# A 32-tile attention loop in eights, written out to all 32 tiles

## The reference

```python
def attn_layer(x, Wqkv, qs, ksc, Wo):
    q, k, v = jnp.split(x @ Wqkv, 3, -1)          # 16 heads of 64
    q = l2norm(q) * qs
    k = l2norm(k) * ksc
    q = q * cos * scale + rotate_half(q) * sin * scale
    k = k * cos * inv + rotate_half(k) * sin * inv
    out = local_attention(q, k, v)                # windows of 32, one back
    return out @ Wo
```

## Time and profile before

| | |
|---|---|
| median of 3 runs | 3703.05 us (3699.27 to 3705.26) |
| the profiled execution's own time | 3708.02 us |
| its span, first to last instruction | 3706.2 us |
| mean granted TensorE clock | 0.947 of full |
| busy: PE, DVE, ACT, POOL | 90%, 72%, 72%, 65% |

### The profile page before, as it was taken

One profiled execution on the slowest core, in us unless ns is written; L12 is line 12 of the kernel. 1 busy time (PEld: TensorE's weight loads), 2 busy tenths in 40 slices (PEclk: granted clock), 3 DMA queues, 4 the chain that ended last, 5 costly groups with the idle time before them and its releaser, 6 DMA issues. The chain is left out here.

```text
span 3706.2 us, 118376 instructions
## 1 busy us (share of the span) xinstructions
PE 3346.1 (90%) x42076; PEld 2217.8 (60%) x42076; DVE 2650.5 (72%) x4986; ACT 2678.7 (72%) x9257; POOL 2404.5 (65%) x2342
## 2 busy tenths in 40 slices
PE   5699998889999789999789999978999977999987
PEld 4466665656666556566566666655666655666656
DVE  6677786577778567778558777756787756777865
ACT  3388887378888458888638888836888854888873
POOL 3577776467777357677547777746777745777764
PEclk8799999899999899999889999989999989999999
DMA  2000001100000100000110000010000010000011
GB/s 67 10 7 7 7 7 32 25 8 7 7 7 5 46 15 7 7 7 7 35 23 7 7 7 6 9 43 14 7 7 7 6 41 18 7 7 7 7 31 42
DMA packets 141063, 57.76 MB, mean 16 GB/s; under 512 B 118598, under 2 KB 137668, under 8 KB 139460
## 3 DMA queue, kind: packets, MB, share of 16 engines
q1 hardware_dynamic: 140484, 50.01, 5.7%
HBM read 22.57 MB, written 2.10 MB: 7 GB/s over the span
## 5 line engine op out<-in xcount | busy, mean ns | idle before, releaser
L1524 POOL TENSOR_TENSOR qk_rot<-by_cos,by_sin 128x1024 f32<-128x1024 f32 x384 | 904.2, 2376 | 234.2 <-PE ring L558 146.2
L1321 ACT ACTIVATE probs<-s_ps,nbias 128x64 f32<-128x64 f32 x3072 | 942.7, 340 | 2.4 <-DVE nbias L1043 2.2
L1001 DVE TENSOR_TENSOR by_cos<-qk_ps,rotary 128x1024 f32<-128x1024 f32 x378 | 463.2, 1225 | 491.6 <-ACT squares L1307 491.6
L612 PE MATMUL ring<-wvo,xsT 128*32 128x512 f32 x6144 | 788.2, 606 | 0.0
L1321 ACT ACTIVATION_READ_ACCUMULATOR probs<-s_ps,nbias 128x1 f32 x3072 | 719.8, 234 | 0.0
L1542 POOL TENSOR_TENSOR qk_rot<-qk_rot,rnorm 128x1024 f32<-128x1024 f32 x192 | 365.7, 1905 | 419.4 <-DVE rnorm L748 419.4
L1513 POOL TENSOR_TENSOR probs<-probs,rrow 128x256 f32<-128x256 f32 x768 | 455.1, 614 | 275.7 <-DVE rrow L988 275.7
L1307 ACT ACTIVATE squares<-qk_ps 128x1024 f32<-128x1024 f32 x378 | 387.3, 1025 | 280.3 <-PE qk_ps L546 280.3
L558 PEld LDWEIGHTS ring<-cst,qk_rot 128*128 128x128 f32 x3072 | 342.8, 140 | 197.0 <-ACT vo L1144 165.8
L1004 DVE TENSOR_TENSOR by_sin<-qk_ps,rotary 128x1024 f32<-128x1024 f32 x378 | 459.2, 1215 | 0.0
L1016 DVE TENSOR_REDUCE sumsq<-squares 128x16 f32<-128x1024 f32 x384 | 455.2, 1185 | 0.0
(11 more groups left out here) (166 smaller groups left out, 5636.7 us busy)
## 6 DMA issues: line engine op xcount, KB each, us to landing
qk_rot<-L_ffn_Wqkv SPq DMA_DIRECT2D x7, 1024.0 KB, 5.0
xs<-x_tok SPq DMA_DIRECT2D x194, 32.0 KB
xs<-x_tok SPq DMA_DIRECT2D x194, 31.8 KB
by_cos<-x_tok SPq DMA_DIRECT2D x48, 128.0 KB
by_cos<-x_tok SPq DMA_DIRECT2D x48, 127.0 KB
wv<-L_ffn_Wqkv SPq DMA_DIRECT2D x7, 512.0 KB, 6.4
wo_pad<-L_ffn_Wo SPq DMA_DIRECT2D x14, 256.0 KB, 7.4
xs<-x_tok SPq DMA_DIRECT2D x194, 0.2 KB
```

The costliest lines, as they stand in the source:

```text
L612: last = mm(r[WIN * mh:WIN * (mh + 1), :], xsT[:, a, WIN * w:WIN * (w + 1)], wvo[:, mh, :, :], start=True, stop=True)
L1001: v.tensor_tensor(heads(by_cos[:, n, :]), heads(projection_banks(qk, k, it, s)), table.unsqueeze(1).broadcast_to([P, H, D]), ALU.mult)
L1321: last = nc.scalar.activation(probs[:, a, h // 4, :, h % 4, :], s_ps[:, half, c:c + 2 * WIN].rearrange("p (s c) -> p s c", s=2), ACT.Exp, ...
L1524: g.tensor_tensor(qk_rot[:, n, :], by_cos[:, n, :], by_sin[:, n, :], ALU.add).then_inc(added[qk], 1)
```

## The change

`schedule` keeps its loop only for the opening block, with two steps a turn as before. The attention of a layer is laid out by a new function, `every_tile`, which has no loop: 35 steps on PE, DVE and ACT and 33 on POOL are written out one after another. Every `step` of the attention loses its `it` argument, tile numbers become `NT * l + k`, and the bank waits come from `last_use` throughout. The order of the operations, their tiles, engines and shapes stay as they were, and so do SP's program, the FFN, and the loop over the layers. The code of a layer's attention grows from 19 to 35 steps on PE, DVE and ACT, and from 17 to 33 on POOL.

```diff
-        def schedule(loop, step, depth, n=NT, after_loop=None, before_last=None, turn=TPB):
-            turns = (n - depth) // turn
+        def schedule(loop, step, depth, n, after_loop=None):
+            turns = (n - depth) // 2
             for k in range(depth):
                 step(k, k % 2, None)
             with loop(0, turns) as it:
-                for r in range(turn):
+                for r in range(2):
                     step(depth + r, (depth + r) % 2, it)
...
+        def every_tile(step, depth, before_last=None):
+            for k in range(NT + depth):
+                if before_last and k == NT + depth - 1:
                     before_last()
-                step(k, k % 2, None)
+                step(k)
+
+        def tile_numbers(l, k):
+            return k, NT * l + k
...
                     def bank(use, s):
-                        i = ring_names.index(use)
                         b = ring_bank((par - s) % 2, use)
-                        if it is not None:
-                            name, s2, ago = use_before(i)
-                            freed(name, T0 - s2 - ago)
-                            if ago and k == 3 and last_use[b][0] != name:
-                                freed(*last_use[b])
-                        else:
-                            if last_use[b]:
-                                freed(*last_use[b])
-                            last_use[b] = use, T0 - s
+                        if last_use[b]:
+                            freed(*last_use[b])
+                        last_use[b] = use, T0 - s
                         return ring[:, b, :]
...
-                schedule(pe.Fori, step, 3, after_loop=after_loop)
+                every_tile(step, 3)
...
-                schedule(dve.Fori, step, 3, before_last=lambda: normalised(0, 0))
+                every_tile(step, 3, before_last=lambda: normalised(0, 0))
...
-                schedule(act.Fori, step, 3, before_last=w1_upper)
+                every_tile(step, 3, before_last=w1_upper)
...
-                schedule(pool.Fori, step, 1)
+                every_tile(step, 1)
```

More of the change, by code:

```diff
@@ L315, in schedule @@
             with loop(0, turns) as it:
-                for r in range(turn):
+                for r in range(2):
                     step(depth + r, (depth + r) % 2, it)
-            k = depth + turn * turns
+            k = depth + 2 * turns
             if after_loop:
@@ L465, in step @@
                     wv_transposed(1, 0)
-            schedule(pe.Fori, step, 4, turn=2, n=NG)
+            schedule(pe.Fori, step, 4, n=NG)
             for r in range(2, WVO_ROUNDS):
@@ L529, in project @@
                     def project(qk, n, s):
-                        if not there(k, it, s):
+                        if not there(k, None, s):
                             return
@@ L575, in scores @@
                     def scores(half, s):
-                        if not there(k, it, s):
+                        if not there(k, None, s):
                             return
-                        t, T, a = t0 - s, T0 - s, (par - s) % 2
+                        T, a = T0 - s, (par - s) % 2
                         first = (k - s) % TPB == 0
@@ L912, in step @@
                 stack_input(5)
-            schedule(dve.Fori, step, 6, turn=2, n=NG)
+            schedule(dve.Fori, step, 6, n=NG)
             with dve.Fori(0, DEPTH) as l:
@@ L1232, in first_wqk_upper @@
                     wqk_upper(0, part)
-            schedule(act.Fori, step, 4, turn=2, n=NG, after_loop=first_wqk_upper)
+            schedule(act.Fori, step, 4, n=NG, after_loop=first_wqk_upper)
             for r in range(2, WVO_ROUNDS):
@@ L1239, in _, with step @@
             with act.Fori(0, DEPTH) as l:
-                def step(k, par, it):
-                    t0, T0 = tile_numbers(l, k, it)
+                def step(k):
+                    (t0, T0), par = tile_numbers(l, k), k % 2
                     def q_evacuated(half, s):
-                        if not there(k, it, s):
+                        if not there(k, None, s):
                             return
@@ L1496, in _, with step @@
             pool.wait_ge(w0_in, 128)
-            schedule(pool.Fori, step, 4, turn=2, n=NG, after_loop=first_weights)
+            schedule(pool.Fori, step, 4, n=NG, after_loop=first_weights)
             step(NG + 4, 0, None)
             with pool.Fori(0, DEPTH) as l:
-                def step(k, par, it):
-                    t0, T0 = tile_numbers(l, k, it)
+                def step(k):
+                    (t0, T0), par = tile_numbers(l, k), k % 2
                     def normalise(half, s):
-                        if not there(k, it, s):
+                        if not there(k, None, s):
                             return
```

43 lines of the change are left out of this document (16 added, 27 removed).

## The result

The changed kernel takes 3640.05 us, the median of 4 runs (3639.45 to 3640.58), where the kernel before, run beside it, took 3701.91 (3699.27 to 3705.26): a ratio of 0.9832, 95% interval 0.9815 to 0.9849. The forecast was 3639.6.

What follows compares the result with a forecast made beforehand. PE, full inside the attention, was taken as the bound. From the 3703.05 us median, 63.4 us for twelve taken PE branches came off, all other terms zero: 3639.6 us, range 3632 to 3646, chance 90%.

Steps and rivals of the forecast that it cites:

- The edges' price: PE's two taken attention-loop branches a layer, twelve in all, cost 63.4 us of stall and lower clock, 5.3 each.
- the lower sum: The twelve PE edges built from idle time plus the half-clock share: 61.7 us, the low end of the saving.
- the twelve edges are of fixed length: PE's attention-loop edges are events of fixed length, so the saving was taken unchanged off the 3703.05 us median.
- The upper sum: The twelve PE edges built from every branch in full plus the clock share: 70.3 us, the high end.
- The other engines' edges: Attention-loop branches on ACT, DVE and POOL: losses lie under PE's stall or within full PE time, so removal wins zero.
- Registers and the loop's set-up: Removing the attention loop's fall-through branch, moves, additions and DVE address registers wins zero, covered by a full PE.
- New fetching: Fetching 16 more steps of straight attention code per engine costs zero; DVE and POOL add some 45 packets in all.
- Rival A: DVE's and POOL's straight attention code is fetched too late, 164 us come back, 3804 us; chance 3%.
- Waits, DMAs: In the attention no wait is added and no DMA moved, so nothing queues behind anything new.
- The layer branch: The layer loop's branch, 4.43 us on PE and taken five times, stays, its target further away: zero change.
- B: The small FFN loops start to miss, giving back 61 us, 3701 us, no change; chance 3%.
- C: TensorE's clock does not stay up in the unbroken attention, losing 41 us, 3680 us, a smaller gain; chance 4%.

Runs made afterwards that it cites:

- Experiment 1: The kernel before, its attention loop entered for two turns of eight steps instead of three, the third turn's steps written out: 3672.76 us, ratio 0.9919.
- experiment 2: The kernel before with six, four or two steps a turn instead of eight: 3725.89, 3836.59 and 3641.55 us; two steps give 78 taken branches.
- experiment 4: The loop of eight kept on some engines, the others written out: PE alone 3700.67 us; DVE, ACT, POOL 3657.62; ACT alone 3655.33; DVE and POOL 3639.70.
- experiment 6: The changed kernel with the loop over the six layers written out too, on all five engines: 3619.42 us, ratio 0.9780.

## Why the prediction was right, point by point

1. *The edges' price, 63.4 us from the starts of line 527.* Right: 64.0 us went from just these intervals, and the medians fell by 61.9 (63.0 against the median shown with the prediction). Experiment 1 halves it with the number of edges. The parts are right too: in these intervals PE was idle for 38.7 us before and for none after, and busy for 25.4 us longer (2436.3 against 2410.9), where the lower sum had 37.9 and 23.8.

The premise that the twelve edges are of fixed length was wrong. The branches of the profiled execution lasted from 3.63 to 5.05 us, and the runs of the kernel before spread over 6.0 us where those of the changed one spread over 1.1. The median of the kernel before itself came out between 3699.36 and 3703.05 us beside the different experiments. That forecast and result lie 0.45 us apart is therefore partly luck; an agreement within 3 or 4 us was what the method could promise.

The upper sum, 70.3 us from whole branches and the clock share, was too high as the text said, and so would be a sum by the Trainium skill's rule for throttled time ("TensorE: Matmul & The Clock Gate", Terms) laid on top of the branches' full durations: what handed-over matmuls cover has to come off.

2. *The other engines' edges lie under PE's: zero.* Right, and the mirror run with PE alone looped shows it (1.0001). The reading behind it was weaker: the 45 ns of ACT's branch record do not say that ACT loses little. On ACT the stall stands behind that record, as its sequencer's two records at the first edge of the kernel before show, 2.5 us apart:

```profile
L315 ACTq COMPARE_BRANCH  x1: 45/45/45, 304.2 to 304.2; - x1
L315 ACTq FUSED_REGOPS  x1: 127/127/127, 306.7 to 306.7; - x1
```

What the text left out is the price of these edges without PE's cover: 15 to 17 us for ACT's, nothing for DVE's and POOL's. A change that wrote out only PE would have been predicted 17.6 us too low (3657.62 against 3640.05).

3. *Registers and the loop's set-up: zero.* Right: the 78 held edges of experiment 2 with all their register work leave PE full, and the 1.5 us that this kernel takes longer are its 288 matmuls more.

4. *New fetching: zero, with some 45 new packets.* The zero is right, the count was not: the second queue went from 211 to 223 packets, 12 more. The runs of experiment 4 take it apart. With DVE and POOL looped and ACT written out the queue has 193, so writing out DVE and POOL adds 30 (I had counted 45), and writing out ACT, which I had put at no new traffic, takes away 18; PE's own queue lost 20 in the same way. Rival A's packets came, 30 of them, and none was exposed: PE stays full.

5. *Waits, DMAs:* no new waits were seen on PE, 387.00 of 387.00 us in layer 1, and 401.8 or 401.9 us for tiles 3 to 31 in all six layers.

6. *The layer branch: zero change.* Right, 4.35 us median against 4.43. That it is worth up to 4.1 us a boundary, the moved table load included, shows only when it is taken away (experiment 6).

The rivals: B did not come, the FFN branch is at 0.22 us as before; with 879, 1280 and 1580 instructions found again, a body of some 200 (203 in the trace) is far from the limit, so its 3% was generous. C did not come either: no fall of the clock between tile 4 and the last in 387 us. PE's busy time fell by 36.1 us where the text had some 20; 25.4 of them are the half-clock part of the edges, 5.7 are in the opening block (87.7 against 82.0 busy) and the rest mostly in the first three tiles of the layers, where the clock fell at other moments in the two executions.

## What to carry to other kernels

When one engine is full and a loop's turns are longer than they must be, look at the duration of its taken COMPARE_BRANCH: on PE 0.2 us was code still at hand, and 3.3 us or more was a fetch, with a further 0, 1.7 or 3.4 us lost to the clock behind it. (On ACT look at what follows the branch, not at its own record.) Then either write the loop out, or make the body small enough: here two steps a turn (879 instructions) came within 1.5 us of 35 written out, and four and six were worse than eight, since they missed more often. Price an edge on every engine by looping that engine alone: the longest stall hides the others until it is gone.

## What the runs showed of the hardware

A taken branch is cheap or dear with nothing between: PE's took 0.21 us with 879, 1280 and 1580 instructions from branch to branch, and 3.3 to 4.3 us with 1753 and 2627 (median of the misses 3.8 and 3.7). On ACT the next instruction began 0.21 to 0.26 us after the branch did with 253 and 377 instructions, and 2.4 us or more with 501; with DVE's 340 it was 0.32 us at most. The Trainium skill, in "Runtime: NRT & Kernel Launch" (Instruction fetch mechanics), gives 2048 instructions for PE and 512 for most of the others. The runs put the usable size below that: 1753 and 501 already miss.

The length of a miss varies: of PE's 12 taken branches before, ten took 3.63 to 3.76 us and two took 4.65 and 5.05. The long ones do not belong to a layer: they fell in layers 3 and 5 there, twice in layer 1 with PE alone looped (4.98 and 4.74), and once in layer 3 in experiment 1 (4.57). I know no reason for them.

Nor does the length of the miss set the time at half clock. In the kernel before the two long branches had 6.8 us of it behind them and the ten others 3.4; but a branch of 4.98 us was followed by 3.4 us (PE alone looped), one of 3.56 us by 6.8 (experiment 1, layer 6), and four of 3.6 to 3.8 us by none (six steps a turn).
